# Two attentions of an eight-block model: the last scores rotate over four PSUM banks, and the last output projection takes half of its contraction ahead

## The reference, cut to what matters

```
scores = einsum('bqhd,bkhd->bhqk', q, k) * scale     # attn0: + bias, causal mask
p = softmax(scores, axis=-1)
ctx = einsum('bhqk,bkhd->bqhd', p, v).reshape(B, S, D)
x = x + ctx @ Wout                                   # attn0: + b_out
```

## Time and profile before

| | us |
|---|---|
| median of 3 runs | 1550.89 |
| lowest and highest | 1548.24, 1556.73 |
| the profiled execution, its own time | 1558.22 |
| its span | 1556.4 |
| TensorE busy | 1384.5 (89%) |
| VectorE busy | 1088.5 (70%) |
| ScalarE busy | 621.3 (40%) |
| GpSimd busy | 329.6 (21%) |
| mean granted TensorE clock | 0.947 |

### The profile page before, as it was taken

The page is one execution under the profiler, slowest core; times in us unless marked ns, Lnnn a source line. Parts: engine busy times, 40 slices in busy tenths (PEclk is TensorE's granted clock), DMA queues, the critical chain, the costliest instruction groups (busy, mean ns, idle before and its releaser), DMA issues. The chain is left out here.

```text
span 1556.4 us, 20758 instructions
## 1 busy us (share of the span) xinstructions
PE 1384.5 (89%) x7632; PEld 971.4 (62%) x7632; DVE 1088.5 (70%) x2216; ACT 621.3 (40%) x1156; POOL 329.6 (21%) x291
## 2 busy tenths in 40 slices
PE   5799999788999989999977999999799889889797
PEld 4455555477888878888851333323377668677676
DVE  5756566498679568887648666676376578888865
ACT  2255545453333333333223555566532334334221
POOL 4211100072433304433322131200022001021010
PEclk9799999799999999999986999999899999999899
DMA  7828330120000000000043250400000000000000
GB/s 153 95 30 109 47 38 2 35 93 1 1 1 1 1 1 1 1 1 1 1 52 57 43 79 28 66 2 1 1 0 1 0 1 0 1 1 1 14 14 27
DMA packets 32319, 39.05 MB, mean 25 GB/s; under 512 B 6002, under 2 KB 27226, under 8 KB 32090
## 3 DMA queue, kind: packets, MB, share of 16 engines
q1 hardware_dynamic: 32218, 37.73, 14.4%
HBM read 14.45 MB, written 2.10 MB: 11 GB/s over the span
## 5 line engine op out<-in xcount | busy, mean ns | idle before, releaser
L1370 DVE TENSOR_REDUCE attn_negm<-ps 128x2 f32<-128x1024 f32 (+3 forms) x256 | 260.2, 1024 | 94.6 <-PE ps L977 53.3
L1190 ACT ACTIVATE attn_probs<-ps 128x512 f32<-128x512 f32 (+3 forms) x512 | 236.8, 515 | 156.3 <-PE ps L1005 82.7
L501 POOL TENSOR_TENSOR moe_h_low<-expert_h,moe_h_high 128x512 fp32r<-128x512 f32 x96 | 137.6, 1435 | 271.4 <-ACT moe_h_high L446 271.4
L997 PE MATMUL ps<-attn_qs,attn_ks 99*128 99x512 bf16 (+4 forms) x512 | 154.3, 352 | 30.3 <-ACT attn_probs L1190 19.4
L977 PE MATMUL ps<-attn_ks,attn_qs 96*128 96x512 bf16 (+4 forms) x512 | 143.6, 364 | 16.9 <-DVE attn_negm L1370 14.8
L464 ACT ACTIVATE moe_silu<-ps 128x512 f32<-128x512 f32 x96 | 57.4, 598 | 200.5 <-PE ps L366 200.2
L1817 PE MATMUL ps<-sb_f_down,tail_h 128*128 128x256 f32 x512 | 122.9, 386 | 7.2 <-DVEq L2108 7.2
L997 PEld LDWEIGHTS ps<-attn_qs,attn_ks 102*128 102x128 bf16 (+1 forms) x512 | 43.9, 98 | 132.2 <-ACT attn_probs L1190 101.1
L1018 PE MATMUL ps<-attn_probs,attn_va 128*32 128x512 f32 (+3 forms) x1024 | 119.6, 541 | 0.0
L1817 PEld LDWEIGHTS ps<-sb_f_down,tail_h 128*128 128x128 f32 x512 | 98.0, 192 | 24.1 <-DVEq L2108 7.3
L2081 DVE TENSOR_TENSOR tail_h<-tail_silu,ps 128x512 f32<-128x512 f32 x64 | 43.6, 682 | 86.1 <-PE ps L1807 54.0
(11 more groups left out here) (350 smaller groups left out, 3252.8 us busy)
## 6 DMA issues: line engine op xcount, KB each, us to landing
attn_qs<-attn_part SPq DMA_DIRECT2D x96, 128.0 KB, 4.6
attn_ks<-attn_part SPq DMA_DIRECT2D x48, 128.0 KB, 7.3
out_x<-x SPq DMA_DIRECT2D x4, 512.0 KB, 2.6
attn_ks<-attn_part SPq DMA_DIRECT2D x24, 64.0 KB, 4.4
x<-in_x SPq DMA_DIRECT2D x2, 512.0 KB, 4.4
x<-in_x SPq DMA_DIRECT2D x1, 1024.0 KB, 10.3
moe_raw<-in_f_down SPq DMA_DIRECT2D x2, 512.0 KB, 6.4
sb_f_gate<-in_f_gate SPq DMA_DIRECT2D x2, 512.0 KB, 4.6
```

The lines of the kernel that those rows point to most:

```text
L501: pool.tensor_tensor(hc.low[:, j % RING, :], h[:, j % RING, :], hc.high[:, j % RING, :], ALU.subtract).then_inc(low_done, 1)
L997: last = pe.matmul(ps[:, SC + k, 0:width2(kt)], ks[0:ROWS2, b % 2, hd % KH, kt * P:(kt + 1) * P], qs[0:ROWS2, b % 2, hd, T - width2(kt):T] ...
L1190: act.activation(pr[:, s2 % RING, j, 0:n], ps[:, SC + k, 0:n], ACT.Exp, scale=HD ** -0.5).then_inc(exp_done, 1)
L1370: dve.tensor_reduce(m, ps[:, 2 * half:2 * half + 2, 0:width1(qt)], AX, ALU.max, negate=True).then_inc(r1_free, 1)
```

## The change

The stage 2 scores of the drain are written to banks 4, 5, 0 and 1 in turn (`DRAIN_SC`, indexed by e % 4, e being the running number of a head's score tile), where before they alternated between 4 and 5. Each matmul waits for the exponential of the tile that was last in its bank (`p2_before`); the first ones in banks 0 and 1 wait until all 128 row maxima have been taken (`r1_free`). For e before the drain, banks and waits come out as before. For the last batch, a new job `out_ahead` for each token half stands at the ends of t = 66 and t = 67: it waits for the first merge's copy and multiplies the first half of the contraction into bank 2 or 3 without closing the sum. `out` for the last batch then adds the second half of the contraction in the same bank; it no longer uses bank 7, so the second `out` no longer waits for VectorE to have emptied the first. The number of matmuls is unchanged.

```diff
--- before.py
+++ after.py
@@ -725,6 +725,7 @@
     LAG, PVLAG = 7, 1
     RING = PVLAG + 2
     SC, CTX, MISC = 4, 6, 7
+    DRAIN_SC, DRAIN_OUT = (4, 5, 0, 1), (2, 3)
     CHUNKS = ["q0", "k0", "q1", "k1"] if causal else ["q0", "k0", "q1"]
     NCH = len(CHUNKS)
     rows_of = {ch: P if causal or ch[0] == "q" else KH * HD for ch in CHUNKS}
@@ -776,6 +777,9 @@
         at[t + 1][1].append(("flip", u))
         if u % 4 in (1, 3):
             at[t + 2][1].append(("merge", u // 4, u % 4 // 2))
+        if u == UNITS - 3:
+            at[t + 3][1].append(("out_ahead", u // 4, 0))
+            at[t + 4][1].append(("out_ahead", u // 4, 1))
         if u % 4 == 3:
             at[t + 3][1].append(("out", u // 4, 0))
             at[t + 4][1].append(("out", u // 4, 1))
@@ -792,8 +796,14 @@
     for both in at:
         for half in both:
             for job in half:
-                if job[0] not in ("high", "context"):
-                    jobs.add(job, MISC, emptied_by(job))
+                if job[0] not in ("high", "context", "out_ahead"):
+                    jobs.add(job, DRAIN_OUT[job[2]] if job[:2] == ("out", B - 1) else MISC, emptied_by(job))
+    p2_bank, p2_before, last_in = [], [], {}
+    for e in range(UNIT * STEPS):
+        bank = SC + e % 2 if e // UNIT < STEPS - LAG else DRAIN_SC[e % len(DRAIN_SC)]
+        p2_bank.append(bank)
+        p2_before.append(last_in.get(bank))
+        last_in[bank] = e
 
     with ExitStack() as stack:
         s = Scope(nc, name, stack, g["to_clear"])
@@ -993,16 +1003,20 @@
                 b = u // 4
                 for k in range(2):
                     hd = UNIT * (u % 4) + 2 * (m % 2) + k
-                    at_least(pe, exp_done, 2 * m + k - 1)
-                    last = pe.matmul(ps[:, SC + k, 0:width2(kt)], ks[0:ROWS2, b % 2, hd % KH, kt * P:(kt + 1) * P],
+                    bank, before = p2_bank[2 * m + k], p2_before[2 * m + k]
+                    if before is not None:
+                        pe.wait_ge(exp_done, before + 1)
+                    elif bank not in (SC, SC + 1):
+                        pe.wait_ge(r1_free, 2 * STEPS)
+                    last = pe.matmul(ps[:, bank, 0:width2(kt)], ks[0:ROWS2, b % 2, hd % KH, kt * P:(kt + 1) * P],
                                      qs[0:ROWS2, b % 2, hd, T - width2(kt):T], start=True, stop=True)
                     if not causal:
                         last.then_inc(s_ready, 1)
 
-            def masks2():
+            def masks2(m):
 
                 for k in range(2):
-                    pe.matmul(ps[:, SC + k, 0:P], identb[:, :], w["mask_kq"][:, :],
+                    pe.matmul(ps[:, p2_bank[2 * m + k], 0:P], identb[:, :], w["mask_kq"][:, :],
                               start=False, stop=True, skip_group_check=True).then_inc(s_ready, 1)
 
             def context(s3):
@@ -1039,9 +1053,24 @@
                     last = pe.transpose(bank[:, t * P:(t + 1) * P], ctx[:, t, c * P:(c + 1) * P], ident[:, :])
                 last.then_inc(ready, 1)
 
+            def out_ahead(b, half):
+                pe.wait_ge(r1_free, 2 * STEPS)
+                pe.wait_ge(free["act"], jobs.count[("merge", b, 0)])
+                for m in range(2):
+                    t = 2 * half + m
+                    pe.matmul(ps[:, DRAIN_OUT[half], m * D:(m + 1) * D], ctxT[:, 0, t * P:(t + 1) * P], w["wo"][:, 0, :],
+                              start=m == 0, stop=False, skip_group_check=True)
+
             def out(b, half):
+                pe.wait_ge(free["act"], jobs.count[("merge", b, 1)])
+                if b == B - 1:
+                    for m in range(2):
+                        t = 2 * half + m
+                        last = pe.matmul(ps[:, DRAIN_OUT[half], m * D:(m + 1) * D], ctxT[:, 1, t * P:(t + 1) * P], w["wo"][:, 1, :],
+                                         start=False, stop=True, skip_group_check=True)
+                    last.then_inc(ready, 1)
+                    return
                 bank = take_bank(("out", b, half))
-                pe.wait_ge(free["act"], jobs.count[("merge", b, 1)])
                 for m in range(2):
                     t = 2 * half + m
                     for c in range(DC):
@@ -1063,6 +1092,8 @@
                     flip(*a)
                 elif kind == "merge":
                     merge(*a)
+                elif kind == "out_ahead":
+                    out_ahead(*a)
                 elif kind == "out":
                     out(*a)
 
@@ -1085,7 +1116,7 @@
                     if 0 <= s2 < STEPS:
                         scores2(2 * s2 + half)
                         if causal:
-                            masks2()
+                            masks2(2 * s2 + half)
                     if s1 < STEPS:
                         scores1(2 * s1 + half)
                         if causal:
@@ -1187,7 +1218,7 @@
                         for k in range(2):
                             j = 2 * half + k
                             act.wait_ge(s_ready, UNIT * s2 + j + 1)
-                            act.activation(pr[:, s2 % RING, j, 0:n], ps[:, SC + k, 0:n], ACT.Exp,
+                            act.activation(pr[:, s2 % RING, j, 0:n], ps[:, p2_bank[UNIT * s2 + j], 0:n], ACT.Exp,
                                            scale=HD ** -0.5).then_inc(exp_done, 1)
                     for job in todo:
                         do(job)
@@ -1342,7 +1373,8 @@
                 if causal:
                     dve.wait_ge(biased, b + 1)
                 xb = x[:, 4 * b + 2 * half:4 * b + 2 * half + 2, :]
-                dve.tensor_tensor(xb, xb, ps[:, MISC, :].rearrange("p (t d) -> p t d", t=2), ALU.add).then_inc(free["dve"], 1)
+                dve.tensor_tensor(xb, xb, ps[:, jobs.bank[("out", b, half)], :].rearrange("p (t d) -> p t d", t=2),
+                                  ALU.add).then_inc(free["dve"], 1)
 
             def do(job):
                 kind, *a = job
```

## The result

The changed kernel takes 1539.84 us (median of 6 runs, 1538.90 to 1540.44) beside 1555.00 us for the kernel before (6 runs, 1548.24 to 1558.59): a ratio of 0.990, 95% interval 0.9879 to 0.9921. That is 15 us less. Run again in a later series, the changed kernel gave 0.9909 (0.9887 to 0.9932) and 1540.78 us.

A forecast was written before the change was run, and what follows sets the result against it. Too few score banks make ScalarE and TensorE wait in turn in the drains; the tails are serial chains. 6.8 + 4.2 + 4.5 + 2.8 - 2.5 = 15.8 us, 1.0%, scaled from 1550.89 to 1535.2 us; range 1529 to 1544.

The forecast's parts named there:

- What held the drains before: Both attention drains: ScalarE and TensorE wait for each other in turn through two score banks, 8.9 and 7.5 us in attn0.
- Drain 0: attn0's drain: four banks cut it from 20.6 to 13.8 us, 6.8 saved; ScalarE's own work a floor of 11.3.
- The walk: TensorE's queue in attn0's drain at 2.4 GHz: ScalarE idles 0.75, 0.2, 0.5 and 0.9 us, 2.4 together.
- Drain 1: attn1's drain: ScalarE becomes the bound, 16.25 + 1.25 = 17.5 us in place of 21.7, 4.2 saved.
- The clock in the drain: attn0's drain: TensorE works closer together, so its clock holds; a fall as before would cost up to 3.4 us.
- Rival (a): New drains: TensorE is the bound, drains save 3.4 + 2.7 us, total 10.9, 1540.0 us; chance 0.15.
- Tails: Behind both drains: only half the projection remains and the first add runs beside it, saving 4.5 us in attn0, 2.8 in attn1.
- The cold start of moe0: Start of moe0: part of the low-clock time moves there from the shortened projection, costing 2.5 us between bounds 0 and 5.2.
- Rival (b): Start of moe0: the low clock's whole stretch moves there, costing 5.2 us; total gain 13.1, 1537.9 us; chance 0.12.
- (c): Drains: banks aren't what holds them, exponentials come no earlier, only the projection gains, 4.8 us, 1546.1 us; chance 0.09.
- (d): From moe0's first transposes: the low clock carried in stays, kernel slower; at 60 us of it 1563 us; chance 0.02.

The follow-up runs named there:

- banks_only: Against the kernel before, only the drains' scores use four banks, the output projection as before: 1544.19 us, ratio 0.9933.
- out_banks_only: Against the kernel before, only a bank for each half of the last output projection, nothing ahead, scores in two banks: one run, 1548.03 us.
- out_only: Against the changed kernel, scores in two banks as before, the projection's first half ahead and a bank for each half kept: 1550.59 us, ratio 0.9974.

## Why the prediction was right, point by point

The median was forecast at 1535.2 and came out at 1539.84 us, inside 1529 to 1544; the gain was forecast at 1.0% and measured at 1.0%, the median of the kernel before being 4 us higher over six runs than over the three shown. The mechanism was the forecast one. That the two percentages agree so closely is in part luck: the terms were off in both directions, and some of the gain is low-clock time of the one execution from which they were read. Stretches at full clock give 18.7 - 14.9 = 3.8 us in drain 0, 3.9 in drain 1 and 2.8 in tail 0; with the same 2.8 for tail 1, an estimate, that is 13.3 us for the change itself.

- **What held the drains before: right.** The mutual waits were the banks. Four banks alone shorten the drains to 13.9 and 16.3 us, and three bring half of four's gain or less.
- **Drain 0, forecast 6.8 us, got 5.7, of which 1.9 were the clock.** The walk came to 13.8 us with 0.9 for the ahead records, so to 12.9 without them; measured were 14.9 and, in banks_only, 13.9. So the ahead records cost what had been counted (1.0 us against 0.9), nearly all of it at t = 67. What failed is the rest of the walk, in two errors that partly cancel. ScalarE idled too little in it: 1.6 us without the ahead records, where banks_only has 13.9 - 10.7 = 3.2. The waits at t = 65 and before the copy were longer (1.04 and 0.70 us, not 0.75 and 0.5), and at t = 67, 69 and 70 it waited 0.40, 0.59 and 0.24 us, for which the walk has nothing. And ScalarE's own work, taken for a floor of 11.3 us, was 10.7.
- **Drain 1, forecast 4.2, got 3.9, from two errors that cancel.** First, the ahead records were costed at nothing, with a step of four exponentials (2.22 us) said to cover a context and four records. The next step's four scores have to fit too: with the ahead records TensorE's step takes 2.92 us (the records start at 1084.03 and 1086.95), and ScalarE waited 0.64, 0.37 and 0.38 us, 1.4 of the 1.5 us by which the drain is longer than without them (17.8 against 16.3). Second, ScalarE's 16.25 us were taken for a floor. With the scores waiting, four exponentials took 2.06 us in place of 2.22, and 15.3 us in all.
- **The clock in the drain: right.** It held at 1.00 in drain 0 in all nine traces with three or more banks. That the banks are the reason is not shown: with two banks it held as well, in out_banks_only and out_only, and fell only in the two traces of the kernel before. Rival (a) had priced the median at 1540.0 us, so the measured median can't tell it from the forecast; the stretches do, since the drains saved 5.7 + 3.9 = 9.6 us where (a) has 6.1. Its premise, TensorE as the bound, was nearer the truth than the forecast had it: in drain 0 TensorE is busy 14.21 of 14.90 us and ScalarE 10.64, and in drain 1 TensorE sets the pace in the steps with ahead records.
- **Tails, forecast 4.5 and 2.8, got 5.2 and 4.3.** The mechanism was right, the size was taken from rows at mixed clocks. At full clock the projection gives 2.8 us in tail 0: 1.1 for the banks, 1.7 for the records ahead. What exceeds it is low-clock time that fell into the tails of the kernel before in its profiled execution; in its second trace tail 0 ran at 1.00 and took 10.1 us. The changed kernel's own tail 0 has 1.7 us of such time in it (8.9 against out_only's 7.2).
- **The cold start of moe0, forecast -2.5, got 0.** moe0's first 14.6 us had a clock of 1.00 and took 14.6 us as before. The low stretch in tail 0 was 3.4 us long ((1 - 0.81) x 8.9 / 0.5) where it had been 10.4, and it ended before moe0. Rival (b) did not come in the changed kernel, in three traces. That it exists is shown by the kernel with three banks, whose low stretch began in tail 0 (clock 0.67 over 9.2 us) and ran on into moe0 (busy time of moe0's first 14.6 us):

```profile
296.60:311.20 14.60, 13.76 (x67) 11.63 (x68) 10.94 (x25) 8.30 (x11) 2.41 (x1) 0.86 0.94 321
```

About (1 - 0.86) x 14.6 / 0.5 = 4.1 us of it were at half, and VectorE's first expert product came 15.8 us into the block, where the changed kernel has it at 14.6: a price of 1.2 us, not 2.5. The Trainium skill, "TensorE: Matmul & The Clock Gate", Part 1, has the half rate released only by sustained activity; the trace agrees there, while in the changed kernel the release came within the eight projection records. The step that failed is the premise of this term, that with half the projection gone part of the low stretch would lie in moe0; the 2.5 was the middle of two bounds and had no row behind it.
- **What was not in the forecast: the blocks between the attentions,** -3.2 us in the pair of profiles. Their time varies from 474.2 to 480.6 us over executions of unchanged code, and from 474.2 to 477.7 for the kernel before alone, so the difference can't be laid to the change. Why the low stretches land in other places each time was not settled; that TensorE's waits at such a place differ (4.36 against 2.72 us) was seen, what comes first was not.

Rivals (c) and (d) fell with the drains and with moe0's clock.

## What to carry to other kernels

Two engines that wait for each other in turn, with neither of them full, want as many buffers as the queue order makes them skip: here four, one for each tile of the step that must stand ready while a longer matmul group holds TensorE's queue; three gave half of four's gain in attn1 and 1.9 of 5.0 us in attn0, and six no more than four. Work taken off a serial tail should go into the tail's own gaps first, where it cost nothing measurable here, before it goes into a stage in which another engine waits for what is queued behind it. For a change of 1%, take its size from stretches at the same clock and from two traces of each kernel, since blocks that nobody touched moved by up to 6 us.

## What the runs showed of the hardware

- ScalarE takes back-to-back exponentials of 128x512 at 2.06 us for four when all scores stand ready, and at 2.22 us when they come just in time (15.3 against 16.25 us busy for the same 32 instructions of attn1's drain); busy time in a starved stage is therefore no floor.
- The same code's low-clock stretches differ from one execution to the next: 6.8 or 3.4 us at half in attn0's drain in two traces of the kernel before, and 474.2 or 477.7 us for the three blocks behind it.
